# Attention stage of a four-block kernel: which scores share PSUM banks, one maximum instruction per pair of banks, and where row statistics stand

## The reference

```python
def _L1_xattn_ref(q, k, v):          # q = layernorm(x), k = v = ctx_512
    NUM_Q_HEADS, NUM_KV_HEADS = 32, 8
    B, S, E = q.shape
    H, KV = NUM_Q_HEADS, NUM_KV_HEADS
    D = E // H                       # 16
    G = H // KV                      # 4
    qh = q.reshape(B, S, KV, G, D).transpose(0, 2, 3, 1, 4)
    kh = k.reshape(B, S, KV, D).transpose(0, 2, 1, 3)
    vh = v.reshape(B, S, KV, D).transpose(0, 2, 1, 3)
    scores = jnp.einsum('bkgsd,bktd->bkgst', qh, kh) / math.sqrt(D)
    weights = jax.nn.softmax(scores, axis=-1)
    out = jnp.einsum('bkgst,bktd->bkgsd', weights, vh)
    return out.transpose(0, 3, 1, 2, 4).reshape(B, S, E)

x = x + jnp.tanh(g_xattn[1]) * _L1_xattn_ref(_layernorm(x, axis=-1), ctx_512, ctx_512)
x = x + jnp.tanh(g_ffn[1]) * _L1_ffn_ref(_layernorm(x, axis=-1), ...)
```

## Time and profile before

| | |
|---|---|
| median of 3 runs | 1863.89 us (1862.64 to 1864.75) |
| profiled execution, its own time | 1867.28 us |
| its span | 1865.5 us |
| PE, DVE, ACT busy over the span | 1512.8, 1321.0, 739.6 us |
| prelude of the attention stage | 806 to 843 us |
| its slots | 843 to 1312 us |
| last feed-forward block | 1316 us to the end |

### The profile page before, as it was taken

One profiled execution on the slowest core, in us unless ns is written; L12 is line 12 of the kernel. 1 busy time (PEld: TensorE's weight loads), 2 busy tenths in 40 slices (PEclk: granted clock), 3 DMA queues, 4 the chain that ended last, 5 costly groups with the idle time before them and its releaser, 6 DMA issues.

```text
span 1865.5 us, 24234 instructions
## 1 busy us (share of the span) xinstructions
PE 1512.8 (81%) x8186; PEld 726.5 (39%) x8186; DVE 1321.0 (71%) x2502; ACT 739.6 (40%) x1060; POOL 467.6 (25%) x438
## 2 busy tenths in 40 slices
PE   2268585792888988348888888989899999999998
PEld 1134343451555555202222222222345444444444
DVE  7887576737699998698887878886555555555555
ACT  5253435222444544305665656657212222222221
POOL 4211121100566666430000000000132323323222
PEclk8589788996999999758999999999999999999999
DMA  5211121113355554452220210212500000000000
GB/s 162 76 30 58 49 64 58 40 46 105 119 161 175 181 168 154 136 135 46 50 53 2 36 22 0 52 23 46 113 1 0 22 0 0 22 0 0 23 11 12
DMA packets 115036, 114.33 MB, mean 61 GB/s; under 512 B 59448, under 2 KB 87352, under 8 KB 114944
## 3 DMA queue, kind: packets, MB, share of 16 engines
q1 hardware_dynamic: 109184, 94.29, 18.3%
q0 software_dynamic: 5760, 18.88, 3.7%
HBM read 59.53 MB, written 31.46 MB: 49 GB/s over the span
## 4 chain that ended last, share of the span: by engine, by line
PE 56%; DVE 30%; DMA 5%; issue 5%; ACT 3%; POOL 1%; SPq 1%; DVEq 0%; ACTq 0%; POOLq 0%
PE PS L1909 17%; PE PS L1932 9%; PE PS L810 6%; PE PS L1384 6%; DVE WORK L1509 6%; PE PS L1363 5%; PE PS L825 4%; PE PS L1372 3%; DVE WORK L1751 2%; DVE WORK L1769 2%; DVE WORK L1752 2%; PE PS L1922 1%; DMA WORK<-in_L_ffn_up_w_dram 1%; DMA WORK<-in_L_ffn_down_w_dram 1%; DVE WORK L1743 1%
## 5 line engine op out<-in xcount | busy, mean ns | idle before, releaser
L1509 DVE TENSOR_REDUCE WORK<-PS 128x1 f32<-128x512 f32 x512 | 326.3, 686 | 71.5 <-PE PS L1363 68.5
L1909 PE MATMUL PS<-BIG 128*128 128x512 f16 x1536 | 342.5, 383 | 8.7 <-DVE BIG L1987 4.6
L1291 ACT ACTIVATE BIG<-PS 128x1024 f32<-128x1024 f32 x256 | 261.6, 1025 | 165.1 <-PE PS L1372 162.8
L1363 PE MATMUL PS<-BIG 128*128 128x512 f16 x512 | 205.5, 404 | 68.9 <-DVE WORK L1509 45.3
L1909 PEld LDWEIGHTS PS<-BIG 128*128 128x128 f16 x1536 | 151.5, 99 | 191.1 <-issue 10.2
L810 PE MATMUL PS<-BIG,WORK 128*128 (+1 forms) x1152 | 184.8, 318 | 4.8 <-DVE WORK L845 4.8
L1932 PE MATMUL PS<-BIG 128*128 128x512 f16 x768 | 173.8, 379 | 1.8 <-DVE BIG L2007 1.8
L1845 ACT ACTIVATE WORK<-PS 128x512 f32<-128x512 f32 x64 | 38.2, 597 | 306.7 <-PE PS L1909 306.7
L1372 PE MATMUL PS<-BIG 128*128 128x512 f16 x512 | 155.3, 387 | 0.1
L1384 PE MATMUL PS<-BIG 128*32 128x512 f32 x1024 | 138.8, 614 | 9.9 <-issue 6.9
L1363 PEld LDWEIGHTS PS<-BIG 128*128 128x128 f16 x512 | 50.1, 98 | 247.2 <-DVE WORK L1509 200.0
(11 more groups left out here) (242 smaller groups left out, 2300.1 us busy)
## 6 DMA issues: line engine op xcount, KB each, us to landing
wdq_scratch<-WORK SPq DMA_DIRECT2D x48, 256.0 KB
WORK<-in_L_ffn_w_dram SPq DMA_DIRECT2D x32, 352.0 KB, 3.6
y_scratch<-WORK SPq DMA_DIRECT2D x40, 256.0 KB, 2.9
BIG<-BIG SPq DMA_DIRECT2D x96, 64.0 KB, 2.3
X<-in_x_dram SPq DMA_DIRECT2D x4, 1024.0 KB, 9.0
WORK<-in_L_ffn_w_dram SPq DMA_DIRECT2D x16, 256.0 KB, 2.7
WORK<-in_L_ffn_gate_w_dram SPq DMA_DIRECT2D x16, 256.0 KB, 3.4
WORK<-in_L_ffn_up_w_dram SPq DMA_DIRECT2D x16, 256.0 KB, 3.6
```

What stands on the lines that cost most here:

```text
L1291: nc.scalar.activation(PB[:, tp, 2 * h:2 * h + 2, :], BPAIR[h % 2], ACT.Exp, scale=SOFT_SCALE).then_inc(exp_ok, 1)
L1363: nc.tensor.matmul(ABANK[i], QS[:, g * HG + h, r * P:(r + 1) * P], KA[:, g, :], start=True, stop=True).then_inc(a_mm, 1)
L1509: v.tensor_reduce(MXU[:, g % 2, c:c + 1], ABANK[i], AX_X, ALU.max, negate=True).then_inc(max_ok, 1)
L1909: ins = nc.tensor.matmul(bank[b], fxT[:, p, a, k * P:(k + 1) * P], w[:, c, l, k, :], start=(i == 0), stop=(i == 3 * KD - 1))
```

## The change

- The scores for the maxima get two pairs of banks, `APAIR[h % 2]`, instead of two single banks. A matmul now waits for the maximum of two slots earlier (one wait a slot). One TENSOR_REDUCE over 128x2x512 with two results takes the place of two.
- The transposed scores get two single banks, `BBANK[j]`, instead of two pairs. Each matmul waits for the exponential taken from its bank one slot earlier, and ACT takes one exponential of 128x512 per matmul: 512 instead of 256. The semaphores count twice as many steps.
- PE's order in a slot becomes A, B, A, B instead of A, B, B, A.
- The four BN_STATS of the finished batch stand in four slots (`ROWS_AT`), the four BN_AGGR and the copy in two more of group 1. For the last batch they stay together at the end.

```diff
-        ABANK, TBANK, OBANK = [bank[0], bank[1]], bank[2], bank[3]
-        BPAIR = [PS[:, 4:6, :], PS[:, 6:8, :]]
+        APAIR, TBANK, OBANK = [PS[:, 0:2, :], PS[:, 4:6, :]], bank[2], bank[3]
+        BBANK = [bank[6], bank[7]]
+        ROWS_AT = [(0, 1, 3), (1, 0, 0), (1, 0, 2), (1, 0, 3)]
...
                         for h in range(HG):
-                            act.wait_ge(b_mm, n * HG + (h + 1))
-                            nc.scalar.activation(PB[:, tp, 2 * h:2 * h + 2, :], BPAIR[h % 2], ACT.Exp,
-                                                 scale=SOFT_SCALE).then_inc(exp_ok, 1)
+                            for j in range(HALF):
+                                act.wait_ge(b_mm, n * 2 * HG + (2 * h + j + 1))
+                                nc.scalar.activation(PB[:, tp, 2 * h + j, :], BBANK[j], ACT.Exp,
+                                                     scale=SOFT_SCALE).then_inc(exp_ok, 1)
...
+                n = u * HG * 2 + (tp * HG + h)
+                if 0 in which and (reuse or tp or h >= 2):
+                    pe.wait_ge(max_ok, n - 1)
                 for i in which:
-                    n = u * HG * R + (tp * 2 * HG + 2 * h + i)
-                    if reuse or tp or h:
-                        pe.wait_ge(max_ok, n - 1)
                     r = 2 * tp + i
-                    nc.tensor.matmul(ABANK[i], QS[:, g * HG + h, r * P:(r + 1) * P], KA[:, g, :],
-                                     start=True, stop=True).then_inc(a_mm, 1)
-
-            def b_slot(n, g, tp, h, first):
-
-                if not first:
-                    pe.wait_ge(exp_ok, n * HG + (h + 1))
-                for j in range(HALF):
-                    t = HALF * tp + j
-                    ins = nc.tensor.matmul(BPAIR[h % 2][:, j, :], KS[:, g, t * P:(t + 1) * P],
-                                           QS[:, g * HG + h, :], start=True, stop=True)
-                ins.then_inc(b_mm, 1)
+                    ins = nc.tensor.matmul(APAIR[h % 2][:, i, :], QS[:, g * HG + h, r * P:(r + 1) * P], KA[:, g, :],
+                                           start=True, stop=True)
+                if 1 in which:
+                    ins.then_inc(a_mm, 1)
+
+            def b_slot(n, g, tp, h, j):
+
+                pe.wait_ge(exp_ok, n * 2 * HG + (2 * h + j + 1))
+                t = HALF * tp + j
+                nc.tensor.matmul(BBANK[j], KS[:, g, t * P:(t + 1) * P], QS[:, g * HG + h, :],
+                                 start=True, stop=True).then_inc(b_mm, 1)
...
             def max_slot(u, g, tp, h):
-                for i in range(2):
-                    n = u * HG * R + (tp * 2 * HG + 2 * h + i)
-                    dve.wait_ge(a_mm, n + 1)
-                    c = h * R + 2 * tp + i
-                    v.tensor_reduce(MXU[:, g % 2, c:c + 1], ABANK[i], AX_X, ALU.max, negate=True).then_inc(max_ok, 1)
+                dve.wait_ge(a_mm, u * HG * 2 + (tp * HG + h + 1))
+                c = h * R + 2 * tp
+                v.tensor_reduce(MXU[:, g % 2, c:c + 2], APAIR[h % 2], AX_X, ALU.max, negate=True).then_inc(max_ok, 1)
...
-                            if tp == 1 and h == 3 and g == 0 and not first:
-                                rows_complete(b - 1)
+                            if not first and (g, tp, h) in ROWS_AT:
+                                rows_stats(b - 1, ROWS_AT.index((g, tp, h)))
+                            if not first and (g, tp, h) == (1, 1, 0):
+                                rows_aggr(b - 1)
+                            if not first and (g, tp, h) == (1, 1, 1):
+                                rows_end(b - 1)
```

35 lines of the change are left out of this document (20 added, 15 removed).

## The result

| | before | after |
|---|---|---|
| median of the runs, same chip | 1863.27 us (1858.58 to 1864.75, 4 runs) | 1828.89 us (1827.27 to 1831.79, 4 runs) |
| ratio, with its 95% interval | 1 | 0.9823 (0.981 to 0.9837) |
| profiled execution, its span | 1867.28 us, 1865.5 us | 1829.95 us, 1828.2 us |

The medians are 34.4 us apart; the forecast's parts summed to 32.2 us, and its time was 1832. The two profiled executions are 37.3 us apart, because the profiled one of before lay 4.0 us above its median and the one of after 1.1.

What follows compares the result with a forecast made beforehand. PE and DVE, waiting for each other in turn for lack of buffers, were taken as the bound. Terms summing to -32.2 us took the profiled 1867.3 to 1835.1; 3.4 less for the median gave 1831.7, rounded to 1832, range 1822 to 1851.

Steps and rivals of the forecast that it cites:

- Rival 3: DVE's maxima: the pair maximum is no cheaper, at 1.52 us, and DVE sets the pace; 1855 us, chance 0.04.
- rival 1: Statistics alone do the work, buffers give little: pair maximum 1.37 us, exponentials of 0.60 without overlap; 1851 us, chance 0.11.
- Plain steps, -7.7: 14 groups of four slot pairs that prepare no next batch: 0.55 us less each, -7.7 us.
- The walk: Following the three engine queues through the slot pairs with the assumed prices; a plain group takes 13.12 us instead of 13.69.
- Preparing steps, -10.3: Nine groups that prepare the next batch: 14.65 to 13.51 us, 1.14 less each, -10.3 us.
- Group 1 to 2, -2.2: The step between these groups: 16.75 to 15.6 us in batch 0, to 16.2 in the others; -2.2 us.
- Statistics and clock, -9.8 and -4.7: Three batch edges: spread row statistics take 16.8 to 13.5 us, -9.8; without PE's idle time the lowered clock goes, -4.7.
- Prelude, -1.8: Opening stretch bound by DVE: two pair maxima take 2.4 us instead of four in 2.67; -1.8 us over 16 slots.
- End of batch 3, +3.7: Groups 6 and 7 with single banks for transposed scores: 22.5 us in all, +3.9, less 0.2 in the step before.
- SP, +0.6: DMAs bringing the next batch's group 0 are wanted 0.7 us earlier: +0.2 us for each of three batches.
- A sign that failed: PE's weight loads would wait under 40 us for maxima, and more than before for exponentials.
- Rival 2: ACT becomes the bound, PE waiting for the same bank's exponential: decides from 0.71 us each, 1873 us at 0.75; chance 0.07.

Runs made afterwards that it cites:

- Experiment 4: The kernel before with one maximum instruction over both of its two banks and no second pair of banks: 1940.55 us in one run.
- experiment 3: The changed kernel with two single maxima per slot in place of one over both banks, pairs of banks and waits kept: 1830.6 us, ratio 0.9817.
- experiments 1: The kernel before with only the row statistics spread over six slots, banks and instructions as before: 1851.84 us, ratio 0.9931.
- 5: The kernel before with only its exponentials split, one bank each, still four banks for transposed scores: 1859.86 us, ratio 0.9988.
- 6: The kernel before with exponentials split and only two banks for transposed scores, the other two unused: 1874.32 us, ratio 1.0073.
- experiment 2: The changed kernel with the row statistics together again in the last slot of group 0: 1837.32 us, ratio 0.9853.
- Experiment 8: The changed kernel with four banks and paired exponentials for transposed scores in groups 6 and 7 of the last batch: 1824.36 us, ratio 0.9801.
- experiment 7: The changed kernel with one exponential of 128x1024 per slot on its one pair of banks, PE's order A, A, B, B: 1894.12 us, ratio 1.0171.
- experiments 11 and 12: The changed kernel with even slots' score order turned and the addition to X one slot later: 1821.11 us; plus four banks ending batch 3: 1818.12 us.

## Why the prediction was right

The forecast was 1832 (1822 to 1851); measured are 1828.9. Some of that closeness is luck: between the profiled executions the parts add up to 37.3 us where the sum had 32.2. Of these 5.1 us only 2.8 show in the times, because I took 3.4 us from the profiled execution to the median and it was 1.1 in the kernel after.

- **The bound and its cure: right.** The forecast read two engines waiting in turn, short of buffers. Experiment 4 shows the lock at its hardest (+76 us with one pair and one instruction) and experiment 3 that the opened lock hardly cares what the maximum costs.
- **The prices: right.** 1217 ns and 598 ns, forecast 1.22 and 0.60. Of a burst, 1.16 us a maximum where I took 1.15. Rival 3 had no chance at 1217, and rival 1 needed 1.37 us and no overlap: two exponentials take 1.08 to 1.11 us together, so the second starts about 0.49 after the first, where I took 0.50. I read the page wrongly: ScalarE: Activation LUTs in the Trainium skill, Rules for kernel authors, gives its 0.3 us for an ACTIVATE whose bias is a pointer operand. These exponentials pass a constant scale and no bias, so 0.72 us was not a figure for them. For an immediate scale and bias the same page, under What ACT_TABLE_LOAD costs, states 186 ns plus 0.833 ns an element, which gives an estimate of 0.61 us for 512 elements, and the 598 ns of this trace agree.
- **Plain steps, -7.7: right in sum, not in detail, and in part by luck.** Measured -8.2, made of -7.2 for the shorter pairs, -1.8 for one thing that I had not seen, and +0.8 for SP. The walk gave 3.29, 3.27, 3.34 and 3.22; measured 3.30, 3.27, 3.23 and 3.21, from the third pair on. The delay of DVE in the fourth pair does not reach PE in the first to the extent that I let it.
- **The loop's jump: missed.** In the kernel before, DVE starts batch 2 after 1.67 us in which it waits for nothing that the profile shows:

```profile
1083.86 2.52 DVE L1509 TENSOR_REDUCE WORK<-PS 128x1 f32<-128x512 f32 x4 [1.67 <-issue]
```

  The step there took 15.41 instead of 13.6, PE idled 1.93 us in it. After the change it takes 13.14, and DVE takes the three maxima around that place (the last of a group, behind `out_add`, and the first two of batch 2) without a gap:

```profile
1061.11 3.48 DVE L1508 TENSOR_REDUCE WORK<-PS 128x2 f32<-128x1024 f32 x3
```

  So the idle time is gone, not hidden by slack. The kept traces separate it from the banks: DVE idles 1.67 to 1.79 us there in the four kernels whose DVE waits twice a slot (before and experiments 1, 5 and 6), and does not in any that waits once a slot, experiment 4 with its single pair of banks and experiment 3 with its two maxima among them. Why the number of waits should matter, no run shows. This term of 1.8 us was to be had from the trace of before: one plain step in fourteen was longer. Without it the plain steps would have come out at -6.4, with SP's 0.8 in it.
- **Preparing steps, -10.3: right** (-10.4).
- **Group 1 to 2, -2.2: too small** (-3.5). I let the statistic and the aggregation that moved there add 0.6 us in two of the three steps. They cost nothing, the step is 15.53 with and 15.56 without them.
- **Statistics and clock, -9.8 and -4.7: right in sum** (-15.4). Experiment 1 measures -12.6 at the edges for the spread alone, and experiment 2 8.6 for undoing it under the new layout. So the two terms are no property of the statistics: the same edit is worth 13 or 8 us, by what slack stands around it. The clock's own price can be read in experiment 2, where 2.21 us of idle time stand once without and once with a fall, and 2.05 us with one: 1.4 to 1.5 us, beside the 1.55 that I took. With the statistics spread, in the kernel after and in experiment 1, the granted clock stays at 1.00 at all three edges. The edges of after take 13.51, 13.51 and 13.35, where the walk said 13.5. The 0.9 us more than forecast lie in the kernel before: I took the first edge's 18.35 for all three, and the second, where the clock stays down for longer, takes 19.35.
- **Prelude, -1.8: too small** (-3.1). Two pair maxima take 2.34 us where I took 2.4, instead of four in 2.67. Eight times that difference is 2.6 us; the other 0.5 I can't attribute. The forecast's own prices, eight times 0.27, would have given 2.2 and not 1.8.
- **End of batch 3, +3.7: right** (+3.9 for the scores). Most pairs take 2.88 us where 2.9 to 3.1 was forecast, and from the first to the last transposed score of the two groups 22.5 us pass, as forecast. Experiment 8 takes 3.0 of it back. The last weight chunk's DMA took 5.57 us instead of 4.94, +0.6 that nothing forecast.
- **SP, +0.6: right in size, wrong in kind.** It was forecast as 0.2 at each of three places. It came as one event of 0.8 in batch 0, told below.
- **A sign that failed:** PE's weight loads were to wait under 40 us for maxima and wait 70 in this stretch. Part of it is harmless: a wait is booked to DVE although PE's previous matmuls are still running, as in the row of 1223.64, where the matmul itself lost 0.23 us. I should have stated the sign in idle time of PE.
- **Rival 2, ACT as the bound: fell by the 598 ns**, and ACT is at the same time the nearest danger: without the split the kernel is 65 us slower than with it (experiment 7).

## What to carry to other kernels

Where two engines show long waits for each other in turn, count the buffers between them before making either faster: here the second pair of banks with all that belongs to it was worth about 28 us, of which the cheaper instruction makes about 3 and the idle time at the loop's jump 1.8. In a kernel like this one buffers should go to the partner that has other work to do in bursts (DVE), taken from the one that has little (ACT), and the latter's instruction split at the buffer's size so that each piece is handed back at once; the split by itself costs nothing here, and without it the changed kernel is 65 us slower. Then keep every other burst shorter than the slack that results, and expect the gains of slack and of smaller bursts to overlap: 28 and 13 us alone, 34 together.

## What the runs showed of the hardware

- **A DMA issue on SP that took 1.68 us.** In batch 0 of the kernel after (timeline 922 to 927 us), one of a row of equal issues took 1.68 instead of 0.63 us, and the matmul that needs the group stood for it:

```profile
922.61 0.59 SPq L1189 DMA_DIRECT2D BIG<-BIG  x1
...
923.25 1.68 SPq L1190 DMA_DIRECT2D BIG<-BIG  x1
...
926.37 0.38 PE L1365 MATMUL PS<-BIG 128*128 128x512 f16 x1 [0.84 <-issue]
```

  The step is 13.77 instead of 13.01. That the matmul waits for this DMA is argued from the order: it is the sixth of the six that bring the group, and the profile names no releaser. In experiment 8 the same issue takes 0.63 us and the step 13.00; experiment 2 has the long issue and 13.76, and experiments 11 and 12 each have such a step in batch 1, 13.85 and 13.70 where its neighbours have 12.74. Long issues are no exception: every one of the 14 traces has two to four of 0.96 to 1.83 us in batches 0 to 2, the kernel before three (1.20, 1.79 and 1.52). What varies is whether one falls among the six that PE needs next, and whether PE has reserve there.
- **One pass over two banks saves DVE little over two passes:** 1217 ns against 2 x 684 when alone, but in a row 1.16 against 1.27 us (two single ones in the trace of experiment 1 took 1.27 or 1.28).
- **The same idle time of PE lets the clock fall in one place and not in another.** 2.21 us: clock 1.00 behind the first edge of experiment 2, 0.81 and 0.62 behind the second. 2.04 and 2.05 us: 1.00 at the loop's jump of experiment 6, 0.59 and 0.84 at the third edge of experiment 2. 1.93 to 1.95 us at the loop's jump: 1.00 in the kernel before and in experiment 1, 0.50 in experiment 5. 3.03 to 3.27 us: lower at every edge of before, but for longer at the second edge of before (0.67, 0.50 and 0.69 in 1099 to 1108 us) than at the first (0.93 and 0.51), and that edge is the longest, 19.35 us. What decides it no run here separates. Where PE idled under 1 us, at the edges of after and of experiment 1, the clock was 1.00. The gain of 0.15 us in each plain step of experiment 5 was 2 us in all, and the fall at its jump took back 1.3 of it.
